# Third softmax's sums with the exponentials as stationary f16 halves, and setup maxima through TensorE, in a one-core sandwich of Nystrom attention and a routed FFN

## The reference

```python
B, N, C = 16, 1024, 256                      # batches, tokens, channels; H = 16 heads, M = 64 landmarks
x = x + layernorm(attention(layernorm(x)))
x = x + layernorm(ffn(layernorm(x)))
# attention
kernel1 = softmax(Q @ K_l.T)                 # N x M   (Q_l, K_l: means over 16 tokens)
kernel2 = softmax(Q_l @ K_l.T)               # M x M
kernel3 = softmax(Q_l @ K.T)                 # M x N
SV  = (kernel1 @ iterative_inv(kernel2)) @ (kernel3 @ V)      # 6 Newton-like iterations
out = SV @ w_proj
# ffn: one of 8 experts is chosen per batch by the reconstruction loss, and its adapter is added
out = x @ W_base + b_base + relu(x @ Wa_down[idx] + ba_down[idx]) @ Wa_up[idx] + ba_up[idx]
```

## Time and profile before

| | |
|---|---|
| three timed runs | 2296.5 us median, 2293.96 to 2301.31 |
| the profiled execution | 2299.66 us, span of the core 2297.9 us |
| busy share of the span | PE 88%, DVE 64%, ACT 37%, POOL 31% |
| mean granted TensorE clock | 0.964 |
| one batch in the steady state | 134.2 us (from 326.23 to 1131.20 us, 6 batches) |
| the score loop in batch 8 | 1169.44 to 1196.7 us |

### The profile page before, as it was taken

One profiled execution on the slowest core, in us unless ns is written; L12 is line 12 of the kernel. 1 busy time (PEld: TensorE's weight loads), 2 busy tenths in 40 slices (PEclk: granted clock), 3 DMA queues, 4 the chain that ended last, 5 costly groups with the idle time before them and its releaser, 6 DMA issues.

```text
span 2297.9 us, 58734 instructions
## 1 busy us (share of the span) xinstructions
PE 2019.7 (88%) x24985; PEld 1307.0 (57%) x24985; DVE 1479.1 (64%) x3330; ACT 861.0 (37%) x1492; POOL 703.4 (31%) x918
## 2 busy tenths in 40 slices
PE   1787999989899998989999898999989899998945
PEld 0464755647475564747556474755647475564724
DVE  2657676676767667676766767676676767767532
ACT  2333434343343434334343434434343343434221
POOL 4026232331513233152323315232331523223051
PEclk9879999999999999999999999999999999999978
DMA  5223222151422215142231514122151422214020
GB/s 124 54 47 81 41 78 63 25 125 30 117 42 77 64 20 130 30 116 43 77 64 24 126 30 118 41 78 63 23 126 30 116 43 77 64 31 100 12 55 19
DMA packets 232971, 150.70 MB, mean 66 GB/s; under 512 B 153035, under 2 KB 203732, under 8 KB 232693
## 3 DMA queue, kind: packets, MB, share of 16 engines
q1 hardware_dynamic: 232710, 146.95, 27.2%
HBM read 36.98 MB, written 16.78 MB: 23 GB/s over the span
## 4 chain that ended last, share of the span: by engine, by line
PE 61%; DVE 17%; SPq 7%; issue 5%; POOL 4%; ACT 3%; DMA 2%; DVEq 1%; POOLq 0%; ACTq 0%
PE NS L942 11%; PE ringF L1150 9%; SPq L424 7%; PE ringF L1135 6%; PE KV L1023 5%; PE ringA L1109 5%; PE ringA L843 4%; PE ringF L1185 3%; PE ringA L1009 3%; PE ringA L985 3%; DVE mx L1485 3%; DVE stage L1575 3%; PE ringF L843 2%; PE ringF L1187 2%; ACT E L686 2%
## 5 line engine op out<-in xcount | busy, mean ns | idle before, releaser
L1150 PE MATMUL ringF<-x,H 128*128 128x256 f16 x1536 | 237.9, 273 | 0.0
L1499 DVE TENSOR_REDUCE mx<-ringA 128x8 f32<-128x512 f32 x256 | 175.6, 686 | 90.1 <-PE ringA L985 89.5
L678 ACT ACTIVATE E<-ringA,score_scale 128x512 f32<-128x512 f32 x256 | 175.6, 686 | 117.4 <-PE ringA L1009 117.2
L843 PE MATMUL ringA<-xT,wqkv 128*128 128x512 f16 x768 | 187.1, 395 | 26.5 <-ACT QS L696 11.7
L1150 PE MATMUL ringF<-H 128*128 128x128 f16 x1024 | 204.4, 220 | 1.4 <-DVE H L1586 1.4
L1552 DVE SCALAR_TENSOR_TENSOR X<-X,NS 128x320 f32<-128x320 f32 x160 | 78.0, 488 | 180.9 <-PE NS L942 175.8
L1485 DVE TENSOR_REDUCE mx<-ringA 128x1 f32<-128x512 f32 x256 | 160.3, 683 | 50.8 <-PE ringA L976 50.2
L1135 PE MATMUL ringF<-wd,x2T 128*128 128x512 f16 x768 | 188.1, 385 | 5.0 <-DVE H L1586 3.4
L513 POOL TENSOR_SCALAR vtmp<-mv,eps_ffn 128x8 f32<-128x8 f32 x16 | 5.1, 318 | 610.4 <-DVE mv L1328 610.4
L686 ACT ACTIVATE E<-ringA,score_scale 128x512 f32<-128x512 f32 x256 | 158.8, 685 | 78.4 <-PE ringA L1040 78.4
L513 POOL TENSOR_SCALAR vtmp<-mv,eps_ln 128x8 f32<-128x8 f32 x32 | 10.0, 312 | 544.3 <-DVE mv L1328 536.6
(11 more groups left out here) (251 smaller groups left out, 4309.3 us busy)
## 6 DMA issues: line engine op xcount, KB each, us to landing
KS<-stage SPq DMA_DIRECT2D x384, 64.0 KB, 2.0
QS<-stage SPq DMA_DIRECT2D x384, 64.0 KB, 2.0
xin<-in_L_attn_x_dram SPq DMA_DIRECT2D x16, 1024.0 KB, 11.0
xres<-in_L_attn_x_dram SPq DMA_DIRECT2D x16, 1024.0 KB, 8.1
out_dram<-yout SPq DMA_DIRECT2D x16, 1024.0 KB, 5.5
QS<-LB SPq DMA_DIRECT2D x16, 512.0 KB, 4.4
E<-in_L_attn_w_qkv_dram SPq DMA_DIRECT2D x1, 768.0 KB, 7.1
H<-in_L_ffn_Wd_dram SPq DMA_DIRECT2D x2, 256.0 KB
```

The lines of the kernel that those rows point to most:

```text
L678: A(E[:, k % ESLOTS, :], ps[:, :], ACT.Exp, scale=score_scale[:, 0:1]).then_inc(freed["s3"].sem, 1)
L843: ins = MM(dst, left(a, k), right(c, k), start=n == 0, stop=n == 3 * KC - 1)
L1150: ins = MM(dst, H[:, a, t, own], src, start=first and i == 0, stop=last and i >= 3, skip_group_check=True)
L1499: V_.reduce_max(mx1[:, t, 8 * h:8 * h + 8], take(b, "m1", k)[:, :].rearrange("p (a m) -> p a m", a=8), AX.X)\
```

## The change

In words: (1) In the score loop ACT takes each bank's exponentials twice, first rounded to f16 (`E16[.., 0, ..]`, four slots that lie in `yout`), then in f32 (`E`); POOL subtracts the one from the other and so makes the low halves. (2) `V` gets f16 halves too (`V16`: low, high, and two ones), by four casts and two subtractions of POOL; `V` itself now lies in the upper four slots of `E`. (3) `sum_values` has the exponentials' halves stationary (128 x 128, f16) and `V16` moving with 65 and 33 columns, three steps behind the scores instead of two, and waits for POOL's low half; the sums land with the landmarks on the partitions, so the transposition and the large reciprocal go. Group 1's sums (k = 8 to 15) use the bank `NS[1]`, so the second kernel's transposition and the inversion's start move to `NS[0]` and `KV`. (4) DVE copies the sums out (`values_take`) and normalises them in four small instructions. (5) `norm1(b+1)` now stands behind POOL's 16 subtractions, and ACT's halves of the next input (L618) go into rounds 1 and 2 of the inversion instead of 0 and 1. (6) Setup: the maxima over the partitions go by a transposition, a DVE maximum and a matmul; the later constants are filled behind `norm1(0)`; `ffn_reduction` goes from DVE to ACT, ahead of its last eight exponentials of batch 0, and the FFN's scales are made in round 3 of the inversion.

```diff
+    VW = 2 * HD2 + 1
+    DM = 272
...
+        E16 = yout[:, :, :].bitcast(F16).rearrange("p t c -> p (t c)").rearrange("p (s h n) -> p s h n", s=4, h=2)
...
-        V = sb("V", [P, T, PAIRS, HD2])
+        V16 = sb("V16", [P, T, PAIRS, 2 * HD2 + 2], F16)
         E = sb("E", [P, ESLOTS, HALF])
+        V = E[:, 4:8, :].rearrange("p k n -> p (k n)").rearrange("p (t a d) -> p t a d", t=T, a=PAIRS)
...
+            def values16(b):
+                for k in range(4):
+                    rows = slice(2 * k, 2 * k + 2)
+                    pool.wait_ge(freed["pv"].sem, freed["pv"].at(b, k + 1))
+                    pool.sem_inc(s_apart, 1)
+                    if k == 0 and not first(b):
+                        pool.wait_ge(kv_full.sem, kv_full.at(b - 1, 2 * T))
+                        pool.sem_inc(s_apart, 1)
+                    pool.tensor_copy(V16[:, rows, :, HD2:2 * HD2], V[:, rows, :, :]).then_inc(v16.sem, 1)
+                for g in range(2):
+                    rows = slice(4 * g, 4 * g + 4)
+                    pool.wait_ge(v16.sem, v16.at(b, 4 + g))
+                    pool.sem_inc(s_apart, 1)
+                    pool.tensor_tensor(V16[:, rows, :, 0:HD2], V[:, rows, :, :], V16[:, rows, :, HD2:2 * HD2],
+                                       ALU.subtract).then_inc(v16.sem, 1)
+
+            def exponentials_lo(b):
+                for k in range(16):
+                    pool.wait_ge(freed["s3"].sem, freed["s3"].at(b, k + 1))
+                    pool.sem_inc(s_apart, 1)
+                    pool.tensor_tensor(E16[:, k % 4, 1, :], E[:, k % ESLOTS, :], E16[:, k % 4, 0, :], ALU.subtract)\
+                        .then_inc(e_lo.sem, 1)
...
                     norm2(b - 1)
+                values16(b)
+                exponentials_lo(b)
                 if more:
...
             norm1(0)
+            later_constants()
             body(0, True)
...
-            pool.wait_ge(s_set.sem, 2)
-            step(pool.partition_all_reduce(amax_all[:, :], amax[:, 0:4], P, bass.bass_isa.ReduceOp.max))
-            assert made[0] == POOL_QKV
...
             def exp3(b, k):
                 ps = take(b, "s3", k)
                 if k >= ESLOTS:
-                    act.wait_ge(kv_full.sem, kv_full.at(b, k - ESLOTS + 1))
+                    act.wait_ge(e_lo.sem, e_lo.at(b, k - ESLOTS + 1))
+                elif k == 4:
+                    act.wait_ge(v16.sem, v16.at(b, 6))
+                if k >= 4:
+                    act.wait_ge(kv_full.sem, kv_full.at(b, k - 4 + 1))
+                elif k == 0 and not first(b):
+                    act.wait_ge(x2lo.sem, x2lo.at(b - 1, 2))
+                A(E16[:, k % 4, 0, :], ps[:, :], ACT.Exp, scale=score_scale[:, 0:1])
                 A(E[:, k % ESLOTS, :], ps[:, :], ACT.Exp, scale=score_scale[:, 0:1]).then_inc(freed["s3"].sem, 1)
...
-                    if more and k < 2:
-                        halves1(b + 1, (k,))
-                    if first(b) and k == 0:
-                        act.wait_ge(s_setpe.sem, 1)
-                        for c in range(KC):
-                            A(f_w2T[:, c, :, :], ringF[c][:, :].rearrange("p (q n) -> p q n", q=EP), ACT.Copy).then_inc(s_w2t.sem, 1)
...
+            pe.wait_ge(s_set.sem, DVE_QKV_MAX)
+            TR(ringF[0][0:4, 0:P], amax[:, 0:4], identf[:, :]).then_inc(s_qkvpe.sem, 1)
+            pe.wait_ge(s_set.sem, DVE_QKV_ROWS)
+            MM(ringF[1][:, 80:84], mxb, identf[0:4, 0:4], start=True, stop=True).then_inc(s_qkvpe.sem, 1)
...
-                pe.wait_ge(freed["s3"].sem, freed["s3"].at(b, k + 1))
+                pe.wait_ge(e_lo.sem, e_lo.at(b, k + 1))
                 if k == 0:
-                    pe.wait_ge(freed["pv"].sem, freed["pv"].at(b, 4))
+                    pe.wait_ge(v16.sem, v16.at(b, 6))
                     if not first(b):
-                        pe.wait_ge(w_done.sem, w_done.at(b - 1, 3))
-                for i in range(2):
-                    for j in range(GP):
-                        p = g * GP + j
-                        ins = MM(KV[32 * j:32 * j + 32, (2 * g + i) * P:(2 * g + i + 1) * P], onesf[:, :] if i else V[:, t, p, :],
-                                 E[:, k % ESLOTS, j * P:(j + 1) * P], start=t == 0 and i == 0, stop=t == T - 1,
-                                 skip_group_check=True)
+                        pe.wait_ge(w_done.sem, w_done.at(b - 1, 4))
+                acc_bank = (KV, NS[1])[g]
+                for j in range(GP):
+                    p = g * GP + j
+                    cols = slice(j * P, (j + 1) * P)
+                    MM(acc_bank[:, j * VW:(j + 1) * VW], E16[:, k % 4, 0, cols], V16[:, t, p, 0:VW], start=t == 0 and j == 0,
+                       stop=False, skip_group_check=True)
+                    ins = MM(acc_bank[:, j * VW + HD2:(j + 1) * VW], E16[:, k % 4, 1, cols], V16[:, t, p, HD2:VW], start=False,
+                             stop=t == T - 1, skip_group_check=True)
                 ins.then_inc(kv_full.sem, 1)
-
-            def values_transpose(b):
-                pe.wait_ge(w_done.sem, w_done.at(b, 2))
-                for g in range(2):
-                    ins = TR(KV[:, g * P:(g + 1) * P], Wt[:, g, :], identf[:, :])
-                ins.then_inc(wt_full.sem, 1)
...
-                    if k >= 2:
-                        sum_values(b, k - 2)
+                    if k >= 3:
+                        sum_values(b, k - 3)
...
+                sum_values(b, 13)
+                if ffn_too:
+                    gram(b - 1, 0, range(0, T // 2))
                 for k in range(14, 16):
                     sum_values(b, k)
-                if ffn_too:
-                    gram(b - 1, 0, range(0, T // 2))
-                values_transpose(b)
...
-            dve.wait_ge(s_setp.sem, POOL_QKV)
+            dve.wait_ge(s_qkvpe.sem, 1)
+            maximum_rows(ringF[0][0:4, 0:P])
+            assert made[0] == DVE_QKV_ROWS
+            dve.wait_ge(s_qkvpe.sem, 2)
...
+            dve.wait_ge(s_setp.sem, POOL_CONSTS)
...
-            def values_normalise(b):
-                dve.wait_ge(kv_full.sem, kv_full.at(b, 2 * T))
-                kv = KV[:, :].rearrange("p (g i n) -> p g i n", g=2, i=2)
-                V_.reciprocal(Wt[:, :, :], kv[:, :, 1, :]).then_inc(w_done.sem, 1)
-                dve.wait_ge(w_done.sem, w_done.at(b, 1))
-                V_.tensor_tensor(Wt[:, :, :], Wt[:, :, :], kv[:, :, 0, :], ALU.mult).then_inc(w_done.sem, 1)
+            def values_take(b, g):
+                dve.wait_ge(kv_full.sem, kv_full.at(b, T * (g + 1)))
+                V_.tensor_copy(kvs[:, 4 * g:4 * g + 4, :], (KV, NS[1])[g][:, 0:GP * VW].rearrange("p (a n) -> p a n", a=GP))                    .then_inc(w_done.sem, 1)
 
             def values_place(b):
-                dve.wait_ge(wt_full.sem, wt_full.at(b, 1))
-                kv = KV[:, 0:2 * P].rearrange("p (a h d) -> p a h d", a=PAIRS, h=2)
-                V_.tensor_copy(X[0:M, :, M:XA], kv[0:M, :, 0, :])
-                V_.tensor_copy(X[M:P, :, M:XA], kv[M:P, :, 1, :]).then_inc(w_done.sem, 1)
+                dve.wait_ge(w_done.sem, w_done.at(b, 2))
+                V_.reciprocal(rden[:, :], kvs[:, :, 2 * HD2])
+                for e in range(2):
+                    rows = slice(e * M, (e + 1) * M)
+                    ins = V_.tensor_tensor(vsum[rows, :, :], kvs[rows, :, e * D:(e + 1) * D],
+                                           kvs[rows, :, HD2 + e * D:HD2 + (e + 1) * D], ALU.add)
+                ins.then_inc(w_done.sem, 1)
+                dve.wait_ge(w_done.sem, w_done.at(b, 3))
+                V_.tensor_tensor(X[:, :, M:XA], vsum[:, :, :], bcast(rden[:, :], D), ALU.mult).then_inc(w_done.sem, 1)
...
-                values_normalise(b)
                 fold1_rows(b)
+                values_take(b, 1)
...
-                if first(b):
-                    ffn_reduction()
```

More of the change, by code:

```diff
@@ L755, in body @@
                         adapter(b - 1)
+                    if first(b) and k == 0:
+                        act.wait_ge(s_setpe.sem, 1)
+                        for c in range(KC):
+                            A(f_w2T[:, c, :, :], ringF[c][:, :].rearrange("p (q n) -> p q n", q=EP), ACT.Copy).then_inc(s_w2t.sem, 1)
                     if 1 <= k < 4:
@@ L770, in body @@
                         ffn_out(b - 1, k)
+                if first(b):
+                    ffn_reduction()
                 for k in range(ESLOTS, 2 * ESLOTS):
@@ L1604, in gram @@
                     dve.wait_ge(freed["gr"].sem, freed["gr"].at(b, q))
+                if first(b) and q == 0:
+                    dve.wait_ge(s_red.sem, 3)
                 V_.tensor_tensor_reduce(out=take(b, "gr", q)[:, 0:GR], in0=bank("gr", q)[:, 0:GR], in1=R2[:, q, :], scale=1.0, scalar=0.0,
@@ L1692, in body @@
                             ffn_sums()
+                        if first(b) and k == 2:
+                            ffn_rows()
+                        if first(b) and k == 3:
+                            ffn_scales()
                 thin_start(b)
```

158 lines of the change are left out of this document (92 added, 66 removed).

## The result

The changed kernel takes 2358.65 us (median, 2354.13 to 2365.11) against 2296.06 for the kernel before: 62.6 us longer, ratio 1.0281 (95% interval 1.026 to 1.0301). The forecast of 2312 had the sign and not the size, and the time lies outside its range. The profiled execution took 2354.13 us, its span is 2351.7. It is the shortest of the four, and the profiled execution of the kernel before (2299.66) is 3.6 us above its median, so the two spans differ by 53.8 us where the medians differ by 62.6.

A forecast was written before the change was run, and what follows sets the result against it. TensorE (PE), busy 88% of the span, was taken to bound most stages. Terms: −15.5 − 8.5 + 1 − 2 + 51 − 16.5 + 6 = +15.5; 2299.7 + 15.5 − 3.2 = 2312 us. Range: a little under 2238 to 2330; forecast alone 2290 to 2335.

The forecast's parts named there:

- The start: Setup up to PE's first projection: without the library routine PE starts near 33.6 us instead of 48.44; −15.5 us taken.
- Batch 0: Batch 0 to 1: ffn_reduction off DVE −8.5 us, FFN scales in DVE's rounds +1, batch 0's score loop −2.
- The fold rows: DVE's fold rows stand behind POOL's two subtractions for V: +3.2 us in each of 16 batches, +51.
- The first rival: At the fold rows, the tiny DVE instructions L1489 and L1495 pass POOL unhindered: 2238 us, chance 0.24.
- The clock ahead of the loop: PE's idle time at the late fold rows lowers its clock behind them: +0.4 us a batch, +6.
- Behind the loop: From the last exponential to ns_first: 5.4 us instead of 6.89, −1.5 a batch.
- The score loop: 15 batches with an FFN around it: −3.1 us if nothing stands in the way; −1.1 a batch taken, −16.5.
- DVE's waits: In the score loop, L1464, L1593 and fold1_rows wait for POOL's subtractions: 0.7 + 0.9 + 0.4 us a batch.
- the last rival: PE's clock falls in the score loop, another 2 us or more a batch: 2340 us and above, chance 0.04.
- In the second half PE is free and ACT becomes the limit: Score loop after k = 5: ACT's two exponentials cost 1.20 us a k; last exponential at 1193.8 instead of 1195.39, −1.6.
- The rule of the Trainium skill: DVE instructions with two SBUF inputs and SBUF-reading GpSimd instructions contend; the first to issue blocks the other; gives the +51.

The follow-up runs named there:

- e1: Changed kernel with POOL's two subtractions for the values' low halves held back until DVE's fold rows are made: 2297.9 us, ratio 1.001 to the kernel before.
- e11: Kernel before with two idle POOL subtractions of 128x1024 added behind norm2, their result never read: 2331.1 us, ratio 1.0153.
- e3: Changed kernel with POOL's 16 subtractions of the exponentials cut to 8 columns, PE reading the high halves instead: 2307.1 us, ratio 1.0054 to the kernel before.
- e9: Changed kernel with late subtractions, K2c's product taking one input from PSUM, and sum_of_squares moved before the last row maxima: 2253.9 us, ratio 0.9816 to the kernel before.
- e12: e9 with six extra PE products of 104 columns at each k from 8 on: 2251.5 us, ratio 0.9804 to the kernel before; 9 us by the trace.

## Why the prediction was right and wrong

- *The start* (−15.5 forecast for the launch): −16.1 at the first fold row. Right, with the split of `w_qkv` colliding as allowed for: POOL's first subtraction takes 3.31 us beside it, 2.12 to 2.29 elsewhere. My 33.6 for PE's start is 1.6 more than the terms named for it give (10.1 + 19.2 + 2.7 = 32.0); measured are 33.09.
- *Batch 0* (−8.5 + 1 − 2, and +3.2 for its fold rows, −6.3 together): −5.5. Right.
- *The fold rows* (+3.2 a batch): +3.19, in all 16 batches, and e1 and e11 show the cause from both sides. The first rival, that tiny instructions pass POOL, did not come true: L1560 took 1.51 us and L1664 1.12. (Its −2.2 a batch should have been −2.0 by my own terms, 3 us of its 2238.) One detail was wrong: the second one held is L1564, a cast with one SBUF input, and not L1566, which L1495 has become; the +3.2 is the same, since the chain goes on when the second subtraction of POOL ends, whichever of the two waits for it. I had written that no DVE instruction with one SBUF input shows this, though L1403 in the earlier trace rows, whose tensor operand is one, does.
- *The clock ahead of the loop* (+0.4): 6.82 − 0.57 − 5.34 = +0.9. I said that DVE hides most of one fall at 1.7 us; where the clock falls, in eleven of 14 batches, it costs 1.15 to 1.33, so DVE hides a third or less.
- *Behind the loop* (−1.5): from the last f32 exponential to `ns_first` 5.17 us instead of 6.88, −1.7. Right.
- *The score loop.* **This is the step that failed, and in it the term for the clock.** The forecast had −3.1 us a batch if nothing stands in the way (1.6 to the last exponential, 1.5 behind it), took 2.0 back for DVE's waits, and had nothing for PE's clock inside the loop: its +0.4 was for the stretch ahead of it. The measured sum is +1.0 instead of −1.1: +2.12 for the loop, −1.7 behind it, and 0.6 because the first f32 exponential is now second in its pair.
  - The gain itself came out. In e3's five batches at full clock the loop takes 23.33 us, 1.93 less than before; with the 0.6 and the −1.7 that is −3.1.
  - What stood in the way was 27.38 − 23.33 = 4.05 us and not 2.0. DVE's waits and the rest of POOL's work are 0.65 + 0.42 + 0.55 = 1.6 of it at full clock, less than my 0.7 + 0.9 + 0.4, though the two instructions grew by what I had said (0.67 and 0.96).
  - The other 2.4 us, by the estimate above, are stretches at 1.2 GHz: the granted clock in the loop is 0.85. I had given that to the last rival with a chance of 0.04, at another 2 us or more a batch and 2340 and above, with the argument that "the loop leaves PE half its time in work". The size that I gave it was right and the chance was not. It is no alternative to the ports either: taking K2c's port away raised the clock from 0.81 to 0.89.
  - "In the second half PE is free and ACT becomes the limit" is neither shown nor refuted. In e3 at full clock ACT is the fullest engine there, and in the ten steps behind the exponential I counted from, the last one starts after 15.70 us, where I had 16.0; but it still waits three times for PE, 1.6 us in all. I had given 2.0 for that.

On the spans' basis the forecast had +2.5 a batch and the trace has +5.1: 2.1 of the 2.6 between them is the loop with its end, 0.5 the clock ahead of it. 14 times 2.6 is 36 us, nearly the 38 by which +15.5 missed +53.7.

The rule of the Trainium skill that I weighed ("SBUF — State Buffer", "Who interferes with whom") is borne out by L1560, L1534 and L1664. The same section says that a `cast` can take the shared ports by itself, in a faster mode; L1564's 2.02 us agree with that. L1591's 0.16 beside POOL's power instruction remains an exception to it.

What stays open: why the granted clock in the loop falls in some batches and not in others of the same text, also in e3 and e9, where PE's waits for the two long DVE instructions are gone; whether ACT's pair bounds a loop without extra products; and how much of e12's 9 us reaches the median.

## What to carry to other kernels

Before work goes to POOL, list the DVE instructions that will run beside it. Here those with two SBUF inputs, a cast and a scaling (L1403) stood until POOL's instruction ended, with L1591 as the exception, and one of eight columns in a dependent chain cost 2 us. The remedies are cheap: put POOL's long instructions behind the short chain, take one input from PSUM, or move the small instruction to where POOL waits. In a loop that hands banks round between three engines, price a wait twice: by what it moves at full clock (0.65 and 0.42 us here, for instructions that were 0.67 and 0.96 us too long), and by TensorE's granted clock after it, which here cost more. The batches of a trace that kept the full clock give the first price without a further run, and they show what extra products for the clock's sake cost themselves.
